# Routing of a half batch behind the key shift, and weight pieces in other steps

## The reference, cut to what matters

```python
q, k, v = x @ Wq.T + bq, x @ Wk.T + bk, x @ Wv.T + bv     # 16 heads of 16
q = softmax(q, axis=-1); k = softmax(k, axis=-2)          # k: over all 1024 tokens of a batch
state = einsum('bhnd,bhne->bhde', k, v)
out = layernorm(einsum('bhnd,bhde->bhne', q, state)) @ Wo.T + bo
x = layernorm(x + out)
x = layernorm(x + cross_attention(ctx, x, mask))          # 77 keys, 8 heads
w, idx = top_k(softmax(x @ router_w), 4)                  # 8 experts; w divided by its sum
y = sum_k w[k] * (gelu(x @ up_w[idx[k]]) @ down_w[idx[k]])  # hidden size 1024
x = layernorm(x + y)
```

## Time and profile before

| | us |
|---|---|
| median of three runs | 1261.82 |
| span of the profiled execution, first to last instruction | 1256.1 |
| time of the profiled execution itself | not listed |
| TensorE matmul busy | 1096.2 (87%) |
| VectorE busy | 764.7 (61%) |
| ScalarE busy | 495.2 (39%) |
| GpSimd busy | 645.5 (51%) |

### The profile page before, as it was taken

How to read it: one execution, slowest core, us unless ns; L and a number is a source line. 1 busy time by engine, 2 the same in 40 slices (tenths; PEclk the granted TensorE clock), 3 DMA queues, 4 the chain that set the end, 5 groups by cost and what they waited for, 6 DMA issues and landing times.

```text
span 1256.1 us, 27061 instructions
## 1 busy us (share of the span) xinstructions
PE 1096.2 (87%) x8572; PEld 904.3 (72%) x8572; DVE 764.7 (61%) x1863; ACT 495.2 (39%) x913; POOL 645.5 (51%) x736
## 2 busy tenths in 40 slices
PE   6568977878887699988899999999999999999960
PEld 3345665656655488877788888888888888888750
DVE  2667978987897687754844444444444444444326
ACT  3754534544343255553233333333333333333214
POOL 3012317756673777766775455555555555554324
PEclk9878979979896799998999999999999999999985
DMA  6421223222212333433444654555544445563326
GB/s 176 154 91 59 93 75 104 74 65 80 77 38 64 72 62 76 71 64 68 65 76 77 134 85 77 77 77 77 77 77 77 77 77 77 77 77 60 64 55 243
DMA packets 163039, 105.07 MB, mean 84 GB/s; under 512 B 107596, under 2 KB 153856, under 8 KB 162656
## 3 DMA queue, kind: packets, MB, share of 16 engines
q1 hardware_dynamic: 132896, 67.67, 21.4%
q0 software_dynamic: 30016, 35.68, 19.7%
HBM read 51.91 MB, written 36.04 MB: 70 GB/s over the span
## 4 chain that ended last, share of the span: by engine, by line
PE 65%; DVE 15%; POOL 9%; issue 5%; DMA 3%; ACT 3%; SPq 0%; POOLq 0%; ACTq 0%; DVEq 0%
PE big L1663 25%; PE big L1682 13%; PE trans L1682 11%; PE big L1705 3%; POOL slot_records L779 3%; PE big L1604 2%; PE small L1751 2%; PE small L1615 2%; POOL early_sums L809 2%; PE trans L1533 2%; POOL rstd L755 1%; PE small L1583 1%; PE big L1707 1%; DVE stat L1047 1%; DVE w_down L1043 1%
## 5 line engine op out<-in xcount | busy, mean ns | idle before, releaser
L1663 PE MATMUL big<-xgT,w_up 128*128 128x256 f16 (+1 forms) x3456 | 408.0, 267 | 12.7 <-DMA xgT<-xg 10.1
L1663 PEld LDWEIGHTS big<-xgT,w_up 128*128 x3456 | 324.7, 98 | 55.9 <-issue 16.4
L902 ACT ACTIVATE h<-big,up_scale 128x512 f32<-128x512 f32 x270 | 185.5, 687 | 451.4 <-PE big L1663 437.6
L1296 DVE TENSOR_SCALAR hh<-h,h_scale 128x512 f16<-128x512 f32 x270 | 133.8, 496 | 312.5 <-ACT h L902 310.8
L809 POOL DMA_INDIRECT token_sums<-y,rec x99 | 163.2, 1649 | 244.5 <-ACT y L910 223.5
L1682 PE MATMUL big<-w_down,hh 128*128 x1264 | 216.8, 274 | 2.8 <-DVE hl L1298 2.5
L1298 DVE SCALAR_TENSOR_TENSOR hl<-h,h_scale,hh 128x512 f16<-128x512 f32 x270 | 203.0, 752 | 9.6
L1682 PE MATMUL big<-w_down,hl 128*128 x632 | 173.0, 274 | 0.0
L1682 PE MATMUL trans<-w_down,hh 128*128 x896 | 152.8, 273 | 2.6 <-DVE hl L1298 2.4
L779 POOL DMA_INDIRECT slot_records<-recs,posi x128 | 130.2, 1017 | 35.3 <-issue 33.6
L1682 PEld LDWEIGHTS big<-w_down,hh 128*128 128x128 f16 x1264 | 123.2, 98 | 20.8 <-issue 3.8
(11 more groups left out here) (249 smaller groups left out, 1512.4 us busy)
## 6 DMA issues: line engine op xcount, KB each, us to landing
w_down<-in_L_ffn_up_w_dram SPq DMA_DIRECT2D x8, 1024.0 KB, 5.0
w_down<-in_L_ffn_down_w_dram SPq DMA_DIRECT2D x7, 1024.0 KB, 5.7
XA<-in_x_dram SPq DMA_DIRECT2D x32, 128.0 KB, 2.6
XRES<-in_x_dram SPq DMA_DIRECT2D x32, 128.0 KB, 2.4
token_rows<-XR SPq DMA_DIRECT2D x32, 128.0 KB, 1.8
sums<-token_sums SPq DMA_DIRECT2D x8, 512.0 KB, 7.2
out_dram<-sums SPq DMA_DIRECT2D x8, 512.0 KB, 2.6
xgT<-xg SPq DMA_TRANSPOSE x135
```

The lines of the kernel that those rows point to most:

```text
L902: act.activation(h[:, i % H_RING, :], psu[up_bank(i)], ACT.Gelu_apprx_tanh, scale=k["up_scale"][:, t:t + 1]).then_inc(gelu_ready, 1)
L1296: dve.tensor_scalar(hh[:, i % HALF_RING, :], h[:, i % H_RING, :], k["h_scale"][:, t:t + 1], None, ALU.mult).then_inc(hh_ready, 1)
L1663: ins = pe.matmul(psu[up_bank(i)][:, j * size(t):(j + 1) * size(t)], w[:, ws, c, m:m + P], xgT[:, t % 2, xs * CC + c, 0:size(t)], start=(n ...
```

## The change

There are two parts. In the steps that close a batch, `routing(s - 1)` is called behind `shift_keys`, and the step ahead of a closing step no longer calls `routing(s)` at its end: choose for the first half of batches 0, 1 and 2 moves from the end of steps 16, 25 and 34 into steps 17, 26 and 35, between shift_keys and norm(2). ACT's shares move behind the exponentials of the keys and the copy of x2T in those steps. In all other steps the order stays. The second part is the list of steps: pieces 8, 9, 12, 13 and 14 are squared in steps 11, 13, 23, 27 and 31 instead of 12, 15, 24, 28 and 32, and piece 11 in step 22 instead of 21. Splits follow one step later each, and loads by L643's formula.

```diff
--- before.py
+++ after.py
@@ -70,7 +70,7 @@
 
 
 
-PIECE_STEPS = [2, 3, 4, 5, 6, 7, 8, 9, 12, 15, 18, 21, 24, 28, 32, 36]
+PIECE_STEPS = [2, 3, 4, 5, 6, 7, 8, 9, 11, 13, 18, 22, 23, 27, 31, 36]
 HALF_STEPS = [TB + 4 + HT * (half + 1) for half in range(HALVES)]
 STEPS = (TB + 1) * (B - 1) + HALF_STEPS[1] + 2
 
@@ -919,6 +919,12 @@
                     act.wait_ge(rows_stored[g % 2], rows_moved(g - 2))
                 act.activation(XR[:, g % 2, 0:C], X2[:, g % 3, :], ACT.Copy, scale=XSCALE).then_inc(hi_ready, 1)
 
+            def routing_shares(s):
+                for half in range(HALVES):
+                    b, i = divmod(s - HALF_STEPS[half] - 1, TB + 1)
+                    if i == 0 and 0 <= b < B:
+                        shares(b, half)
+
             copy_turned(xT, "x", 0)
             for s in range(MIX0):
                 a, after = first_tile(s), first_tile(s + 1)
@@ -938,10 +944,8 @@
                     copy_turned(x1T, "x1", c2, XD ** -0.5)
                 if after is not None:
                     copy_turned(xT, "x", after)
-                for half in range(HALVES):
-                    b, i = divmod(s - HALF_STEPS[half] - 1, TB + 1)
-                    if i == 0 and 0 <= b < B:
-                        shares(b, half)
+                if closing(s) is None:
+                    routing_shares(s)
                 if a is not None:
                     act.wait_ge(qs_ready, a + 1)
                     act.activation(Q[:, a % TB, :], Q[:, a % TB, :], ACT.Exp).then_inc(qe_ready, 1)
@@ -959,6 +963,8 @@
                 if c4 is not None:
                     high_rows(c4)
                     copy_turned(x2T, "x2", c4)
+                if closing(s) is not None:
+                    routing_shares(s)
                 if c2 is not None and s < MIX0 - 1:
                     exp_logits(c2)
                 if square_piece(s) is not None:
@@ -975,10 +981,7 @@
                     copy_turned(qT, "q", c0)
                 if c3 is not None:
                     exp_logits(c3)
-                for half in range(HALVES):
-                    b, r = divmod(s - HALF_STEPS[half] - 1, TB + 1)
-                    if r == 0 and 0 <= b < B:
-                        shares(b, half)
+                routing_shares(s)
                 if c2 is not None:
                     copy_turned(x1T, "x1", c2, XD ** -0.5)
                 gelu(i + 1)
@@ -1406,6 +1409,7 @@
                     moments(1, c1)
                 if close is not None:
                     shift_keys(close)
+                    routing(s - 1)
                 if c4 is not None:
                     norm(2, c4, X2[:, c4 % 3, :], x2_ready)
                 if c2 is not None:
@@ -1430,7 +1434,8 @@
                     build_state(close)
                 if piece is not None:
                     split_low(piece)
-                routing(s)
+                if closing(s + 1) is None:
+                    routing(s)
                 if s == COUNT_STEP:
                     dve.tensor_copy(early_counts[:, :], small_wait(("early",))[:, 0:EXP]).then_inc(sm_free, 1)
                 if s == MIX0 - 2:
```

## The result

The changed kernel takes 1272.26 us (median of 5 runs, 1270.46 to 1274.48), the kernel before in the same job 1261.45 (5 runs): ratio 1.0073, interval 1.0045 to 1.0102. It is slower by about 9 us; 1263.4 had been forecast, the range ended at 1269.5.

A forecast was written before the change was run, and what follows sets the result against it. DVE was taken to bound the kernel up to about slice 13, TensorE's expert matmuls afterwards. Terms -4.3 -4.7 -0.5 +1.1 +1.1 -0.5 -1.6 +7.5 +3.5 summed to +1.6: span 1257.7, time 1263.4 us, range 1256 to 1269.5.

The forecast's parts named there:

- The bound: Closing steps: two limits, DVE until X2 and half-clock PE from kb on, both ending at the state's products; PE last.
- PE's lag: Closing step 17: PE ended 1.5 us behind DVE's way to X2, time the change was to win back.
- It saves that way nothing: Closing step 17: choose only moves across kb on DVE's way to X2, so it doesn't shorten that way.
- -4.3, -4.7 and -0.5: Terms in us for closing steps 17, 26 and 35, each faster through an earlier kb.
- The wait, +7.5 +3.5: Steps 23 and 24: ScalarE waits for piece 12's late load, +7.5 us; PE's half clock behind it, +3.5.
- Piece 12 split in 24 instead of 25: +1.1: Step 24: cost in us of a piece in an otherwise plain step, bounds 0 and +2.6.
- Piece 11: -0.5: Moved a step later, it leaves a step where gates already runs: -0.5 us, bounds -1.4 to +0.5.
- Piece 9 in steps 13 and 14: +1.1 (bounds 0 and +2.6): Cost in us of its square and split in those steps, at the price of a piece in a plain step.
- Piece 13: -1.6: Its split leaves step 29 and partly uses DVE's idle time in step 28: -1.6 us, bounds -2.9 to -0.3.
- Rival (d): Closing steps give PE's lag alone, -3.0 instead of -9.5 us, so 1269.9; chance 0.08.
- Rival (b): Wait at step 24 costs more than its length, half clock lasting into the next step: 1268.4 us; chance 0.20.

The follow-up runs named there:

- e2: Changed kernel with the old list of steps, so only choose behind shift_keys is left of the change: 1263.90 us, 1.0020 against the kernel before.
- e7: Changed kernel with the old list of steps and choose just ahead of build_state in closing steps: 1256.04 us, 0.9950 against the kernel before.
- e10: As e2, but choose one place later, right behind norm(2): 1263.99 us, 1.0022 against the kernel before.
- e12: e7 plus 27 filler transposes of the identity on PE in each closing step, in four places: 1250.55 us, 0.9919 against the kernel before.
- e3: Changed kernel, but piece 12's load waits for 11 splits instead of 12: 1262.04 us, 0.9992 against the kernel before.
- e8: e3 plus 14 filler transposes of the identity on PE ahead of x2's turn in closing steps: 1265.94 us, 1.0013 against the kernel before.
- e11: New list of steps, piece 12's load free of the wait, choose just ahead of build_state in closing steps: 1253.74 us, 0.9947 against the kernel before.
- e14: e11 with the wait of piece 12's load put back as in the changed kernel: 1263.22 us, 1.0017 against the kernel before.
- e1: Kernel before with the change's list of steps alone, routing in its old place: 1269.75 us, 1.0058.
- e6: Kernel before with only pieces 8 and 9 moved, to steps 11 and 13 instead of 12 and 15: 1268.02 us, 1.0051.
- e9: Kernel before with the new list of steps and piece 12's load waiting for one split fewer, routing untouched: 1266.75 us, 1.0045.
- e16: Kernel before with only piece 9 moved, to step 13 instead of 15: 1265.25 us, 1.0032.
- e4: Kernel before with only pieces 11 and 12 moved, to steps 22 and 23: 1272.90 us, 1.0080.
- e13: e4 with piece 12's load waiting for one split fewer: 1267.61 us, 1.0041 against the kernel before.
- e5: Kernel before with only pieces 13 and 14 moved, to steps 27 and 31 instead of 28 and 32: 1263.60 us, 1.0010.

## Why the prediction was wrong, by its own steps

**The bound.** "DVE until X2, and PE at half clock from the kb product on, which ended last by 1.5 us": this is the step that failed. DVE's limit on the state's products is not X2 but L1350, 2.8 us behind X2 in the changed kernel (171.00 to 173.78). In all 15 closings at steps 17, 26 and 35 of five kernels in which PE's own routing product was done by then (the change, e2, e7, e10, e12) the products start 0.09 to 0.11 us behind its end, and so they do in the 12 of e3, e8, e11 and e14. In the kernel before that operation is L1347:

```profile
172.25 0.42 DVE L1347 TENSOR_TENSOR X<-small,xr 128x256 f32<-128x256 f32 x1
```

It ended at 172.67 at step 17, and PE started the products at 173.29, 0.62 us behind. At step 26 that is 0.62 too, at step 35 only 0.10. So PE's lag, the thing I wanted back, was 0.5 us at steps 17 and 26 and nothing at 35, not 1.5. e10 against e7 shows it: X2 at the same time (166.27 and 166.35), choose ahead of or behind L1350, products at 172.20 or 169.66, and 9 us of run time between them (1.0022 and 0.9950).

**"It saves that way nothing".** That sentence on choose was right and I did not carry it through: I still let kb's 4.3 us reach the products. e2, with choose moved and the splits left, gains 2.6 us at kb of step 17, counted from V's copy of step 16, and 0.9 at the products. The closings gave -1.9, -1.8 and -1.9 instead of -4.3, -4.7 and -0.5; where choose truly leaves the way (e14, the same list), V's copies and the first gelu show -5.0, -4.8 and -3.3. At closing 17, from V's copy of step 16 to that of 18, the new list with choose in its old place gives -2.9 to -3.6 (e1, e6, e9, e16), choose behind shift_keys with the old list -0.5 (e2), and both together -1.9 to -2.2 (the change, e3, e8). So behind shift_keys choose took back a part of what the split's absence gives.

**The wait, +7.5 +3.5.** Right in mechanism, and near in the place's total partly by luck. From V's copy of step 23 to that of 25, the four kernels with the wait (the change, e1, e4, e14) lose 10.6 to 11.4 us against before; my terms with piece 12's +1.1 make 12.1. But the five without it (e3, e8, e9, e11, e13) lose 3.6 to 5.1 there, so the wait itself is 6 to 7 us of it. Its first part was well sized: up to V's copy of step 24 the kernels with the wait lose 8.1 to 8.7 us, those without it 0.5 to 0.9. The +3.5 for the clock behind it was not: from there to step 25 they lose 1.9 to 2.9, and those without the wait 2.7 to 4.3. A clock term that was too large and the next term, which was too small, made up for each other.

**"Piece 12 split in 24 instead of 25: +1.1", with "Piece 11: -0.5".** Mis-sized. Two steps with a split stand side by side. e13 has only that (it also takes piece 12's split out of the step ahead of closing 26, which gives 0.6 us in its trace). It costs 5.2 us by its runs, where these terms give 0.6. PE's pause in step 24 and the granted clock:

```profile
249.83 1.10 PE L1583 MATMUL small<-woT,zT 128*128 128x256 f32 x4 [2.31 <-DVE wcl L1029]
...
248.00:250.00 2.00, 0.17 (x1) 0.20 (x2) 1.90 (x8) 0.35 (x1) 1.58 (x4) 1.00 0.04 5
250.00:252.00 2.00, 2.00 (x10) 1.85 (x10) 1.90 (x9) 1.58 (x2) 0.55 (x1) 0.73 0.02 1
252.00:254.00 2.00, 2.00 (x5) 0.60 (x4) 0.57 (x4) 1.44 (x4) 1.61 (x4) 0.50 0.19 66
```

(The last three lines: window, its length, busy us of PE, PEld, DVE, ACT, POOL, the clock, DMA.) Piece 11's split takes 2.78 us (243.86) at the end of step 23; PE then pauses 2.31 us ahead of the projection of step 24 (249.83), released by DVE's scale of piece 12, and its clock falls. I had priced a piece by the mean length of steps whose neighbours have none.

**"Piece 9 in steps 13 and 14: +1.1 (bounds 0 and +2.6)."** The trace has +1.75, within the bounds. By its runs, though, e16, whose sum with the closing's gain I put at -1.2, loses 4.0. Its splits of pieces 8 and 9 are neighbours again, but that this is the cause is not shown: its trace has the loss in later steps that were not changed.

**"Piece 13: -1.6."** Not confirmed: e5, which moves it and piece 14, is at 1.0010, with an interval that still holds -1.6 us. In the trace the stretch 27 to 34 got 4.6 us longer. Of this 3.0 us also stand in e2 and in e4, in which these pieces were not moved, while e9 and e11, in which they were, lose only 0.7 there. The granted clock falls twice in it after the change (0.52 in 306 to 308, 0.50 in 350 to 352), and in the kernel before the windows around it are at 1.00; so most of the 4.6 us can't be laid to these pieces, and what makes the clock fall there stays open.

**Rivals and range.** Rival (d), closings worth PE's lag alone beside a wait of the forecast size, gave 1269.9, 2.4 us from what came, and had 0.08: the nearest in time, and half right: the closings gave 5.6 us in the trace, where I had 9.5. That is 3.9 of the 7.6 us that the runs lie above my sum (9.2 against 1.6). Another 2.9 is the late two pieces by e5's ratio (+1.3 against -1.6), which isn't clear of noise; the pair of splits is no part of the miss, since with the wait its place came 0.7 us under my terms. Rival (b) had the sign and 0.20, but the clock is back at 0.96 in the window 260 to 262 of the changed kernel, within step 24, so its mechanism isn't what did it. The range ended 0.4 us short of (d), and 2.8 short of what came.

**What adds and what doesn't.** List (e9, +5.7) and routing (e2, +2.5) cost 8.2 apart and -1.0 together (e3); with the list the wait is worth 10 (change against e3), 9 (e14 against e11), 5 for the pair alone (e4 against e13), but 1.6 in e1 against e9. The traces have its 6 to 7 us in steps 24 and 25 in each. The list without the wait costs 5.7 in e9 and nothing in e11 against e7. What evens this out elsewhere was not settled: e16 shows that a fall of the clock in an unchanged step is worth 3 us, and such falls differ from kernel to kernel.

## The clock at the closing steps

e12 against e7 shows the price of the half clock apart from all else. In e7 the four windows of 2 us from 166 to 174 have a granted clock of 0.66, 0.50, 0.50 and 0.63, in e12 1.00 throughout; the state's products take 1.84 us less, and V's copy of step 18 gains 1.85 us from that of step 16 on. TensorE's page of the Trainium skill ("TensorE: Matmul & The Clock Gate", its list of terms) prices such a stretch at its length times one minus the granted share, by which the four windows would be worth 3.4 us. The trace says 1.85: part of the stretch PE waits for DVE at either clock, and the products start 0.10 us behind L1350 in both. At steps 26 and 35 they take 3.81 us too, against 6.74 and 5.45 in e7. Yet over the whole kernel e12 gains only 3.9 us on e7 by the ratios (0.9919 and 0.9950), and since the two intervals overlap, that sum is not clear of noise. The trace shows where some of it goes: behind closing 17 e12 loses 1.7 us again in step 19, where its clock falls and e7's stays at 1.00:

```profile
184.00:186.00 2.00, 2.00 (x5) 1.10 (x5) 1.51 (x5) 1.65 (x4) 1.80 (x2) 0.50 0.72 192
```

In the closing steps themselves the fillers delay nothing that shows.

## What to carry to other kernels

Before an operation is moved ahead of or behind another on the same engine, list everything further down that other engines wait for, the reads that free a shared PSUM bank included: an operation leaves the path only if it ends up behind the last of them, and a pause marked "issue" with all operands there can be such a bank, as it was here. A buffer that is refilled only after its last reader needs as many steps between two uses as load and reader take; two uses in neighbouring steps put the load on the path, and here the two heavy steps side by side cost 5.2 us even without it (e13). Where a TensorE pause can't be removed, harmless matmuls can keep 2.4 GHz for the work behind it: 14 in one gap, with pauses of 1.98 and 1.31 us left behind them, gave nothing (e8); 27 over four gaps, which left no pause over 0.72 us behind kb, held the clock at 1.00 from kb to the end of the state's products in all three closings and gave about 4 us (e12). Parts of a change that were measured alone need not add up: those of the list came to 17.8 us alone and to 7.3 together.

## What was unexpected in the hardware

Equal pauses did not have equal effect: behind 0.98 and 1.71 us without work in step 19 the granted clock fell to 0.50 in e16, as it did behind the same pauses in e1 and e9, and stayed at 1.00 in the kernel before and in e6; e16 and the kernel before are 3.0 us apart for it. What decides it was not found. The runs of one and the same kernel spread by some 10 us (kernel before, 27 runs of one job: 1257.35 to 1268.8), so a single pair of profiles can be off by 5 us in its sum, as the 14.2 us here against 9 measured.
